# A gated low-rank tile turned in 32x32 blocks on VectorE, first products ordered by kinds, and other PSUM banks for the last tile

## The reference

```python
z      = einsum('bct,bcd->bdt', x, W[condition])         # x: 128 x 64 x 1024 float32
base   = z @ W_base.T + b_base                           # 1024 -> 1024
logits = z @ W_gate.T                                    # 8 experts
top_p, top_i = top_k(softmax(logits), 2);  top_p /= sum(top_p)
h      = einsum('bnd,erd->bner', z, A)                   # 8 experts x rank 16 = 128 values
out    = x + base + einsum('bner,eor->bno', h * route_w, B)
```

## Time and profile before

| | us |
|---|---|
| three runs | 947.12, 947.48, 949.1 |
| median | 947.48 |
| the profiled execution | 946.93 |
| its span, first to last instruction | 945.2 |

### The profile page before, as it was taken

The page is one execution under the profiler, slowest core; times in us unless marked ns, Lnnn a source line. Parts: engine busy times, 40 slices in busy tenths (PEclk is TensorE's granted clock), DMA queues, the critical chain, the costliest instruction groups (busy, mean ns, idle before and its releaser), DMA issues.

```text
span 945.2 us, 16847 instructions
## 1 busy us (share of the span) xinstructions
PE 938.7 (99%) x5474; PEld 882.7 (93%) x5474; DVE 427.7 (45%) x1328; ACT 380.2 (40%) x810; POOL 535.5 (57%) x506
## 2 busy tenths in 40 slices
PE   8999999999999999999999999999999999999998
PEld 7999999999999999999999999999999999999997
DVE  5784344443444433444434444344444344443444
ACT  6463343434334333334334343333443343434332
POOL 3575547655566555575555665455655546655560
PEclk9999999999999999999999999999999999999999
DMA  9522332233322233332333222333223332233312
GB/s 303 188 79 101 133 113 98 89 111 122 133 89 94 95 122 133 111 96 92 108 125 128 94 86 103 122 133 107 89 88 115 133 112 99 89 111 122 133 49 86
DMA packets 41453, 107.15 MB, mean 113 GB/s; under 512 B 4449, under 2 KB 8674, under 8 KB 41442
## 3 DMA queue, kind: packets, MB, share of 16 engines
q1 hardware_dynamic: 41440, 107.01, 32.9%
q10 hardware_dynamic: 2, 0.00, 0.0%
HBM read 73.43 MB, written 33.55 MB: 113 GB/s over the span
## 4 chain that ended last, share of the span: by engine, by line
PE 97%; DVE 1%; DMA 1%; ACT 0%; SPq 0%; issue 0%; DVEq 0%
PE ps L787 54%; PE ps_r L787 19%; PE ps_out L805 11%; PE ps_out L815 9%; PE ps L846 3%; PE ps_hwt L811 1%; DMA w_sum<-in_w_t 1%; DVE w_sum L603 1%; PE ps_r L846 1%; DVE o_sb L633 0%; PE ps L832 0%; PE ps_r L832 0%; ACT a_hi L413 0%; DVE w_lo L596 0%; ACT w_hi L425 0%
## 5 line engine op out<-in xcount | busy, mean ns | idle before, releaser
L311 POOL TENSOR_TENSOR a_lo<-raw,a_hi 128x512 fp32r<-128x512 f32 x128 | 166.1, 1317 | 247.7 <-ACT a_hi L413 247.7
L620 DVE TENSOR_TENSOR z_sum<-ps,z_sum 128x448 f32<-128x448 f32 x150 | 93.7, 624 | 241.1 <-PE ps L787 241.1
L787 PE MATMUL ps<-w_hi,s_hi 128*128 128x448 f32 x480 | 177.6, 370 | 0.0
L787 PE MATMUL ps<-w_lo,s_hi 128*128 128x448 f32 x480 | 175.5, 366 | 0.0
L787 PE MATMUL ps<-w_hi,s_lo 128*128 128x448 f32 x480 | 173.6, 362 | 0.0
L787 PE MATMUL ps_r<-r_lo,a_hi 128*128 128x264 f32 x496 | 140.9, 284 | 0.0
L787 PE MATMUL ps_r<-r_hi,a_hi 128*128 128x264 f32 x496 | 140.6, 284 | 0.0
L787 PE MATMUL ps_r<-r_hi,a_lo 128*128 128x264 f32 x496 | 140.5, 283 | 0.0
L787 PE MATMUL ps<-w_hi,a_hi 128*128 128x448 f32 x360 | 134.0, 372 | 0.0
L787 PE MATMUL ps<-w_lo,a_hi 128*128 128x448 f32 x360 | 131.1, 364 | 0.0
L633 DVE TENSOR_TENSOR o_sb<-ps_out,o_sb 128x448 f32<-128x448 f32 (+1 forms) x192 | 94.3, 506 | 80.9 <-PE ps_out L815 80.7
(11 more groups left out here) (96 smaller groups left out, 1629.8 us busy)
## 6 DMA issues: line engine op xcount, KB each, us to landing
raw<-in_x_t SPq DMA_DIRECT2D x128, 256.0 KB, 2.8
o_sb<-in_x SPq DMA_DIRECT2D x64, 512.0 KB, 3.9
out_x<-o_sb SPq DMA_DIRECT2D x62, 512.0 KB, 2.6
w_sum<-in_w_t SPq DMA_DIRECT2D x8, 448.0 KB, 9.2
r_raw<-in_w_t SPq DMA_DIRECT2D x4, 264.0 KB, 5.5
table_raw<-in_cond_w SPq DMA_DIRECT2D x2, 256.0 KB, 8.8
b_raw<-in_b_t SPq DMA_DIRECT2D x1, 512.0 KB, 11.0
out_x<-o_sb SPq DMA_DIRECT2D x2, 224.0 KB, 2.2
```

What stands on the lines that cost most here:

```text
L311: pool.tensor_tensor(a_lo[j][:], raw[j][:], as_f32(a_hi[j][:]), ALU.subtract).then_inc(s_a_lo[j], 1)
L620: return dve.tensor_tensor(to, bank[:, 0:NS], other, ALU.add)
L787: mm = pe.matmul(bank[:, 0:w.shape[-1]], a[:, k, :], w[:, k, :], start=(opens and k == 0 and q == 0), stop=(closes and k == KH - 1 and q = ...
```

## The change

Three parts. **Turning.** In every step, turn_hw(2p - 1) is gone from TensorE. DVE turns hw of tile 2p + 1 right behind weigh_experts(p, 1), at the end of pair 1 and of every step but the last, by 16 transposes of 32x32 that write hwt_sum (which has the memory of hwt_lo); ACT casts hwt_hi and DVE subtracts hwt_lo from there. Tiles 0, 1, all even tiles and tile 63 are turned on TensorE as before. **Opening.** The products with the first half of R's weights and those with B11 are made kind by kind (HH, LH, HL), in quarters of two k, each group behind the wait for what it reads. **The last tile.** L of tile 63 is made in ps_6, and Q in ps_1; mix_chunk(31, 1, L) comes before R half 0; the end of DVE's program is reordered (finish), and ACT writes the seeds into these banks.

```diff
-        hwt_lo = sb("hwt_lo", [P, P], F32R)
+        hwt_sum, hwt_lo = shared("hwt_sum", "hwt_lo", [P, P])
...
 # ACT
+            def turned_hwt_top(p):
+                act.wait_ge(s_turned, BLOCKS * p)
+                act.copy(hwt_hi[:], hwt_sum[:]).then_inc(s_hwt_hi, 1)
...
             def step(p, last):
...
-                hwt_top(2 * p - 1)
+                turned_hwt_top(p - 1)
...
                 added_top(p, 1, L)
-                hwt_top(2 * p)
+                if last:
+                    act.copy(ps_6[:, 0:NS], bias[:, cols(L)]).then_inc(s_seed[L], 1)
+                hwt_top(p + 2)
                 added_top(p, 0, Q)
+                if last:
+                    act.wait_ge(s_z_lo[0][L], p + 1)
+                    act.copy(ps_1[:, 0:NS], bias[:, cols(Q)]).then_inc(s_seed[Q], 1)
+                    exps(2 * p + 1)
+                    seed(p, 1, R)
+                    return
                 seed(p, 1, L)
-                if last:
-                    seed(p, 1, R)
-                    exps(2 * p + 1)
-                    seed(p, 1, Q)
-                    return
...
 # DVE
+            def turn_hw(i):
+                dve.wait_ge(s_hw, i + 1)
+                for c in range(P // TURN):
+                    for r in range(P // TURN):
+                        dve.transpose(hwt_sum[c * TURN:(c + 1) * TURN, r * TURN:(r + 1) * TURN],
+                                      hw[r * TURN:(r + 1) * TURN, c * TURN:(c + 1) * TURN]).then_inc(s_turned, 1)
...
             def step(p, last):
                 dve.wait_ge(s_p1_out, p - 1)
                 dve.wait_ge(s_p[6], p + 1)
                 add(ps_6, p1, u2).then_inc(s_u2, 1)
-                hwt_rest(2 * p - 1)
+                hwt_rest(2 * p - 1, hwt_sum[:])
...
+                if last:
+                    finish(p)
+                    return
                 output(p, 0, L)
                 added_rest(p, 0, Q)
                 output(p, 0, R)
                 rank_experts(p, 1)
-                if last:
-                    weigh_experts(p, 1)
-                    output(p, 0, Q)
-                    return
                 z_rest(p, 1, R, ps_r[:, 0:width[R]])
                 output(p, 0, Q)
                 weigh_experts(p, 1)
+                turn_hw(2 * p + 1)
+
+            def finish(p):
+                added_rest(p, 0, Q)
+                rank_experts(p, 1, ps_6)
+                weigh_experts(p, 1)
+                output(p, 0, L)
+                output(p, 0, R)
+                hwt_rest(2 * p + 1)
+                output(p, 0, Q)
+                z_rest(p, 1, R, ps_r[:, 0:width[R]])
+                output(p, 1, L, ps_6)
+                output(p, 1, Q, ps_1)
+                output(p, 1, R)
...
 # TensorE
-            for piece in range(2):
-                first_r(ps_r, 0, piece)
-                first_r(ps_5, 1, piece)
-            first_q(ps_1, 0, 0, "B11").then_inc(s_p[1], 1)
-            first_q(ps_6, 1, 0, "B11").then_inc(s_p[6], 1)
+            def first_kind(bank, t, j, kind, u_hi, u_lo, n):
+
+                u, v = ((a_hi, u_hi), (a_hi, u_lo), (a_lo, u_hi))[kind]
+                for k in range(2 * j, 2 * j + 2):
+                    mm = pe.matmul(bank[:, 0:n], u[2 * t][:, k, :], v[:, k, :], start=(k == 0 and kind == HH),
+                                   stop=False)
+                return mm
...
+            pe.wait_ge(s_a_hi[A11], 1)
+            pe.wait_ge(s_r_hi, 1)
+            r_kind(0, 0, HH)
+            pe.wait_ge(s_a_lo[A11], 1)
+            r_kind(0, 0, LH)
+            pe.wait_ge(s_r_lo, 1)
+            r_kind(0, 0, HL)
+            pe.wait_ge(s_a_hi[A21], 1)
+            r_kind(1, 0, HH)
+            r_kind(1, 0, HL)
+            pe.wait_ge(s_r_hi, 2)
+            r_kind(0, 1, HH)
+            r_kind(0, 1, LH)
+            r_kind(1, 1, HH)
+            pe.wait_ge(s_a_lo[A21], 1)
+            r_kind(1, 0, LH)
+            r_kind(1, 1, LH)
+            pe.wait_ge(s_r_lo, 2)
+            r_kind(0, 1, HL)
+            r_kind(1, 1, HL)
+            for j in range(2):
+                pe.wait_ge(s_w0_hi["B11"], j + 1)
+                for t in range(2):
+                    b11_kind(t, j, HH)
+                    b11_kind(t, j, LH)
+                pe.wait_ge(s_w0_lo["B11"], j + 1)
+                for t in range(2):
+                    mm = b11_kind(t, j, HL)
...
                 strassen(ps_6, s2_hi, s2_lo, T2, True).then_inc(s_p[6], 1)
-                turn_hw(2 * p - 1)
...
                 lora(0, L)
                 lora(0, R)
+                if last:
+                    mix_chunk(p, 1, L, ps_6)
                 pe.wait_ge(s_a_lo[A21], p + 1)
                 plain_r(ps_r, 1, 0, True, False)
-                mix_chunk(p, 1, L)
                 if not last:
+                    mix_chunk(p, 1, L)
                     plain_r(ps_r, 1, 1, False, True).then_inc(s_r_sum[1], 1)
                 mix_chunk(p, 0, Q)
                 lora(0, Q)
...
+            turn_hw(2 * p + 1)
             plain_r(ps_r, 1, 1, False, True).then_inc(s_r_sum[1], 1)
-            turn_hw(2 * p + 1)
-            mix_chunk(p, 1, Q)
+            mix_chunk(p, 1, Q, ps_1)
             pe.wait_ge(s_hwt_lo, 2 * p + 2)
-            lora(1, L)
-            lora(1, Q)
+            lora(1, L, ps_6)
+            lora(1, Q, ps_1)
```

More of the change, by code:

```diff
@@ L23 @@
 A11, A12, A21, A22 = range(4)
+TURN = 32
+BLOCKS = (P // TURN) ** 2
 WARM_UP = 10
@@ L184, in adaln_ffn @@
         s_hw = sem("hw_ready")
-        s_hwt = sem("hwt_ready")
+        s_hwt = sem("hwt_in_psum")
+        s_turned = sem("hwt_blocks_turned")
         s_hwt_hi = sem("hwt_hi_ready")
@@ L487, in _ @@
             a_top(1, A11)
-            hwt_top(0)
+            hwt_top(1)
             act.wait_ge(s_p[3], 1)
@@ L504, in first @@
                 z_top(0, L, ps_1[:, 0:NS])
-                hwt_top(1)
+                hwt_top(2)
                 t_top(1, T1)
@@ L517, in first @@
                 z_top(0, R, ps_r[:, 0:width[R]])
-                hwt_top(2)
+                hwt_top(3)
                 t_top(4, NT4)
@@ L578, in _ @@
             pairs(act, first, step)
-            hwt_top(TILES - 1)
+            hwt_top(PAIRS + 2)
             act.wait_ge(s_r_sum[1], PAIRS)
@@ L735, in first @@
                 weigh_experts(1, 1)
+                turn_hw(3)
             def step(p, last):
@@ L798, in plain_r, with mix_chunk @@
                                opens, closes)
-            def mix_chunk(p, t, c):
+            def mix_chunk(p, t, c, bank=None):
                 pe.wait_ge(s_z_lo[t][c], p + 1)
@@ L804, in mix_chunk @@
                 for q, (m, z) in enumerate(((0, z_hi), (0, z_lo), (1, z_hi))):
-                    mm = pe.matmul(ps_out[c][:, 0:width[c]], mix[t][:, m, :], z[t][:, cols(c)],
+                    mm = pe.matmul((bank or ps_out[c])[:, 0:width[c]], mix[t][:, m, :], z[t][:, cols(c)],
                                    start=False, stop=(q == 2), skip_group_check=True)
@@ L811, in turn_hw, with lora @@
                 pe.transpose(ps_hwt[:, 0:P], hw[:], ident[:]).then_inc(s_hwt, 1)
-            def lora(t, c):
+            def lora(t, c, bank=None):
                 for q, (h, b) in enumerate(((hwt_hi, b_hi), (hwt_hi, b_lo), (hwt_lo, b_hi))):
-                    mm = pe.matmul(ps_out[c][:, 0:BASE_COLS[c]], h[:], b[:, base(c)], start=False,
+                    mm = pe.matmul((bank or ps_out[c])[:, 0:BASE_COLS[c]], h[:], b[:, base(c)], start=False,
                                    stop=(q == 2), skip_group_check=True)
@@ L849, in first_q, with r_kind, b11_kind @@
                 return mm
-            for piece in range(2):
-                first_r(ps_r, 0, piece)
-                first_r(ps_5, 1, piece)
-            first_q(ps_1, 0, 0, "B11").then_inc(s_p[1], 1)
-            first_q(ps_6, 1, 0, "B11").then_inc(s_p[6], 1)
+            HH, HL, LH = range(3)
+            def first_kind(bank, t, j, kind, u_hi, u_lo, n):
[4 more added lines that the diff above has]
+                return mm
+            def r_kind(t, j, kind):
+                return first_kind((ps_r, ps_5)[t], t, j, kind, r_hi, r_lo, width[R])
+            def b11_kind(t, j, kind):
+                return first_kind((ps_1, ps_6)[t], t, j, kind, w_hi[:, B11], w_lo[:, B11], NS)
+            pe.wait_ge(s_a_hi[A11], 1)
[26 more added lines that the diff above has]
+                    mm = b11_kind(t, j, HL)
+                    if j == 1:
+                        mm.then_inc(s_p[(1, 6)[t]], 1)
             first_r(ps_r, 0, 2)
```

16 lines of the change are left out of this document (8 added, 8 removed).

## The result

| us | before | changed | ratio [95%] |
|---|---|---|---|
| median | 948.37 (947.12 to 949.1, 6 runs) | 943.48 (942.72 to 943.86, 6 runs) | 0.9949 [0.9937, 0.9962] |
| profiled execution | 946.93, span 945.2 | 942.72, span 941.0 | |

Faster by 4.8 us, from 3.6 to 6.0 by the interval. The forecast was 943.2 us, and its gain 4.3. (The median before is 948.37 over six executions; the forecast started from the 947.48 of the first three.)

A forecast was written before the change was run, and what follows sets the result against it. TensorE, busy 99% of the span, was taken as the bound. Gains of 3.45 (loop), 0.30 (opening) and 0.56 (tail) sum to 4.31: 946.93 becomes 942.6, plus 0.55 to the median gives 943.2 us; range 941.8 to 944.7.

The forecast's parts named there:

- loop, 30 transposes: Loop steps: 30 transposes leave TensorE at 0.115 us each, a gain of 3.45 us (3.3 to 3.6).
- opening: Before the first mix product: TensorE arrives 1.1 us sooner but waits for ACT's seed, held by the bias; gain 0.30 us.
- tail: Last tile: TensorE's wait before Q, 0.48 us, and the 0.08 restart go; gain 0.56 us (0.3 to 0.6).
- The bound: From first loop step to last pair TensorE never waits, so only instructions taken from it shorten the step.
- No gain in the loop: Rival: something else sets the step's 28.99 us and the removed slot becomes a wait; 946.6 us, chance 0.06.
- The price of a transpose: On TensorE in the loop: a removed transpose is worth its successors' shift, 0.115 us (0.11 to 0.12).
- The rival at the whole 0.27: Rival: each removed transpose saves its whole 0.27 us, 8.1 us in all; 938.5 us, chance 0.02.
- The blocks: DVE at each step's end: 16 block transposes take 3.5 us in 4.38 us of idle time and cost nothing.
- The deadline: Worked back from TensorE's lora(1, L): blocks may end as late as 511.0 us; each us past costs one per step.
- Late blocks: Rival: DVE's blocks, locked out by POOL's subtractions, end 0.8 us past the deadline; 24 us slower, 967 us, chance 0.05.
- the wait of some 0.7 us before a first mix product at 27.6: Sign in the opening: TensorE waits some 0.7 us for ACT's seed and starts the first mix product at 27.6.
- TensorE starting near 5.9: Sign in the opening: first products need only r_hi, cast by 5.74, so TensorE starts near 5.9 instead of 6.63.

The follow-up runs named there:

- turn_only: The kernel before with the turning part of the change alone; 944.4 us, ratio 0.9961 to the kernel before.
- blocks_24: The changed kernel with 8 more block transposes, into an unused tile, in each tile that DVE turns; 943.71 us, ratio 0.9957 to the kernel before.
- blocks_32: The changed kernel with 16 more block transposes, into an unused tile, in each tile that DVE turns; 992.96 us, ratio 1.0472 to the kernel before.
- both_turned: The changed kernel with tile 2p of pairs 2 to 30 turned on DVE too, and lora(0, L), (0, R) and mix_chunk(p, 1, L) moved later; 1004.89 us.
- opening_only: The kernel before with the first products by kinds (the opening part) alone; 947.03 us, ratio 0.9989 to the kernel before.
- bias_early: The changed kernel with the bias load issued ahead of B22 instead of behind pair 1's rows; 943.1 us, ratio 0.9945 to the kernel before.
- both_psum: Against both_turned: tile 2p's blocks go to PSUM in groups of 4, 8, 4, z_lo(1, Q) moves behind output(p, 0, R), bias loaded early; 942.16 us.

## Why the prediction was right

| term, us | forecast (ends) | by the traces | its part alone, by times |
|---|---|---|---|
| loop, 30 transposes | 3.45 (3.3, 3.6) | 3.00 | 3.7 (2.5 to 5.0) |
| opening | 0.30 (0, 1.1) | 0.70 (one execution) | 1.0 (0.2 to 1.9) |
| tail | 0.56 (0.3, 0.6) | 0.50 | 1.1 (0.3 to 2.0) |
| sum | 4.31 | 4.2 | 4.8 for the whole (3.6 to 6.0) |

The mechanism held in all three places, and two of the three sizes were off. The sum holds partly by luck: two errors cancel, 0.45 too much for the loop and 0.40 too little for the opening of the profiled execution. The time itself, 943.48 for 943.2, is closer than the gain, 4.8 for 4.3, since the kernel before measured 948.37 beside it and not 947.48. And the upper end of the range does not follow from its working: 943.9 and the named scatter of 1.6 make 945.5, not 944.7. The result lies inside either.

- **The bound** held: no wait in 843.5 us of TensorE. "No gain in the loop" is out: turn_only alone gives 2.9 us in its 29 steps. TensorE does 34 transposes, as forecast.
- **The price of a transpose** is the term that was mis-sized: 0.100, outside my ends of 0.11 and 0.12. I compared 24 products with a transpose with 24 products elsewhere in the step, and the chain's slot; the neighbours of the removed instruction also shift a little when it goes. In the changed kernel, P6 and P2 run from 504.84 to 509.70, 4.86 us, where the rows had 4.97; the lora group behind them takes 1.41 instead of 1.40. The rival at the whole 0.27 is out: 28.893 and not 28.72. So is what the Trainium skill's 275 ns (TensorE: Matmul & The Clock Gate, Part 4) would have made of it: its figure, given for bf16, is the duration, and the slot was 0.10.
- **The blocks** were priced at 16 x 0.22 = 3.5 and took 3.72. They go one at a time, 0.2325 apart, which a copy of another shape could have told only by chance; the estimate was near because the duration that I took, 0.22, happens to lie near the distance. The deadline was right: blocks_24 ends on the near side of it and blocks_32 on the far side.
- **Late blocks**, the slower rival, had a real mechanism on the wrong instruction. In the changed kernel POOL's two subtractions run from 503.54 for 2.55 us beside the blocks, and these keep their 3.72. But DVE's subtractions of two SBUF inputs are held up by POOL, as both_turned shows. The turning has one such subtraction, hwt_lo from 508.01 to 508.29, and it fell where POOL was idle, between two of its casts (the one before ended at 507.87, the next started at 508.35). In all 30 steps it took 0.28. That it was this placing that kept the change safe is argued from both_turned; I had not looked at it, so here the forecast was lucky. I had argued from hw's product, which reads PSUM as well.
- **The opening**: its logic was right (seed start + 0.68, restart 0.08), its size was not, since I fixed the seed at the 26.96 of one execution. It started at 26.61 in the changed kernel, 27.34 in opening_only, 27.35 in turn_only, and up to 28.32 in blocks_32. So the wait of some 0.7 us before a first mix product at 27.6, which I had named as a sign, did not come in the changed kernel's profile (0.20, at 27.29), and came in opening_only's (0.69, at 28.02). TensorE itself comes 0.7 to 1.1 sooner (27.33, 27.09, 26.88 in opening_only, the changed kernel and bias_early, for 28.02). "TensorE starting near 5.9" was 5.35, since r_hi is cast from a load that also varies. The range for this term, 0 to 1.1, was the useful answer: opening_only's trace shows 0, the changed kernel's 0.70 and bias_early's 1.1. Why the times give 1.0 for opening_only when its trace gives nothing is not resolved; its 0.2 to 1.9 allows most of these values, and the executions of opening_only do spread less (946.58 to 948.16) than those of before beside them (946.9 to 950.61).
- **The tail**: the wait of 0.48 and the restart of 0.08 went, and 0.06 is missing, spread over the slots of other products: each half of R for tile 63, with new neighbours, takes 1.48 in the chain.

## What to carry over

On a saturated TensorE, price a small instruction by how far its successors move, not by its duration, and take off a little for neighbours that shift; work moved to another engine is free up to a deadline that can be worked out back from its consumer, and costs one for one per step past it (one kernel past it was measured). Before placing DVE work beside POOL's, look at which DVE instructions get pushed against POOL: those with two SBUF inputs waited it out in both_turned. Moving them away from POOL's work mended it here; whether moving one operand to PSUM would do it alone was not tested. A gain in an opening that ends at a transfer is as variable as the transfer, so read several executions or issue it sooner. And look behind the last product too: both_psum gained 2.26 us on TensorE and 0.7 in the span, because its last store landed late.

## What was not expected of the hardware

- A 32x32 float32 block transpose on DVE lasts 203 ns and starts 0.2325 us behind the last one when its partitions change, 0.10 when they stay (then 157 ns); extra blocks that change place but send no semaphore start 0.215 apart. Into PSUM it lasts 224 ns.
- 128x128 hwt_lo of two SBUF inputs took 1.34 us beside POOL and 0.28 alone; block transposes were not stretched beside POOL (all 944 of both_turned lasted 199 to 208 ns).
- The transpose on TensorE, 0.27 us long, was worth 0.10 in one place of the step and 0.067 in another (where the order around it changed as well).
